# Attention in a fused transformer block: score buffers of three and four banks in turn, one bank for sums and turned sums

## What is computed

```
h = _layernorm(x) * (1 + ca) + sa
q, k, v = h @ Wq + bq, h @ Wk + bk, h @ Wv + bv          # 16 heads of 16
mask = cols <= rows + WINDOW                             # WINDOW = 128
scores = einsum('bhqd,bhkd->bhqk', q, k) / sqrt(16)
attn = softmax(where(mask, scores, -inf), axis=-1)
out = einsum('bhqk,bhkd->bhqd', attn, v)
x = x + ga * (out.transpose(...).reshape(b, s, d) @ Wo + bo)
```

## Time and profile before

| what | value |
|---|---|
| time, median of 3 runs | 1954.98 us (1951.56 to 1959.11) |
| the profiled execution | 1954.75 us |
| its span, first to last instruction | 1951.9 us |
| attention, first score matmul to last step | about 187 to 1260 us |
| PE busy over the span | 1763.1 us (90%) |
| ACT busy over the span | 1576.9 us (81%) |

### The profile page before, as it was taken

The page is one execution under the profiler, slowest core; times in us unless marked ns, Lnnn a source line. Parts: engine busy times, 40 slices in busy tenths (PEclk is TensorE's granted clock), DMA queues, the critical chain, the costliest instruction groups (busy, mean ns, idle before and its releaser), DMA issues. The chain is left out here.

```text
span 1951.9 us, 46416 instructions
## 1 busy us (share of the span) xinstructions
PE 1763.1 (90%) x18739; PEld 989.3 (51%) x18739; DVE 598.2 (31%) x1462; ACT 1576.9 (81%) x2077; POOL 266.1 (14%) x325
## 2 busy tenths in 40 slices
PE   7944999999999998999999999878399999999995
PEld 5732333333333333333333333266288888888884
DVE  6953000000000000000000000056466676776772
ACT  5623899999999998999999999834288888888882
POOL 1000100001010001000010000027312222222211
PEclk9965999999999999999999999977599999999998
DMA  5464400004000004000010000096422222222223
GB/s 178 146 161 107 93 10 10 10 10 88 23 11 10 10 12 92 10 10 10 10 27 18 10 2 2 26 369 221 144 36 36 37 39 36 37 39 37 37 39 100
DMA packets 83037, 112.47 MB, mean 58 GB/s; under 512 B 9340, under 2 KB 75836, under 8 KB 82236
## 3 DMA queue, kind: packets, MB, share of 16 engines
q1 hardware_dynamic: 65768, 86.65, 16.0%
q0 software_dynamic: 13296, 17.80, 5.4%
q10 hardware_dynamic: 3760, 5.03, 0.9%
HBM read 72.90 MB, written 40.74 MB: 58 GB/s over the span
## 5 line engine op out<-in xcount | busy, mean ns | idle before, releaser
L1144 ACT ACTIVATE at_probs<-at_scores 128x1536 f32<-128x1536 f32 (+2 forms) x756 | 1022.6, 1436 | 52.6 <-PE at_scores L1045 47.2
L1045 PE MATMUL at_scores<-at_q_rows,kept_k_rows 99*32 99x512 bf16 (+3 forms) x9920 | 616.0, 361 | 33.6 <-ACT at_probs L1144 17.0
L1062 PE MATMUL at_out<-at_probs,kept_v 128*17 128x512 f32 (+3 forms) x4832 | 586.1, 564 | 5.1 <-DVE at_out_T L1157 4.7
L1045 PEld LDWEIGHTS at_scores<-at_q_rows,kept_k_rows 99*32 99x32 bf16 x9920 | 238.1, 96 | 556.4 <-ACT at_probs L1144 344.6
L1157 DVE COPY at_out_T<-at_out 128x512 f32<-128x512 f32 x32 | 22.1, 691 | 967.0 <-PE at_out L1062 967.0
L1776 PE MATMUL ex_ps_y<-kept_w,kept_mixed 128*128 x1136 | 258.6, 381 | 2.4 <-ACT kept_mixed L1837 2.4
L1776 PEld LDWEIGHTS ex_ps_y<-kept_w,kept_mixed 128*128 128x128 f32 x1136 | 211.4, 191 | 28.9 <-issue 2.7
L1129 POOL TENSOR_SCALAR_AFFINE_SELECT at_probs<-at_probs 128x512 f32<-128x512 f32 (+2 forms) x156 | 83.0, 541 | 1003.9 <-ACT at_probs L1144 1001.9
L1837 ACT ACTIVATE kept_mixed<-ex_ps_hT,kept_b 128x128 f32<-128x128 f32 x568 | 154.6, 384 | 78.5 <-PE ex_ps_hT L1768 78.5
L1062 PEld LDWEIGHTS at_out<-at_probs,kept_v 128*17 128x17 f32 x4832 | 127.6, 98 | 130.0 <-DVE at_out_T L1157 20.4
L1862 DVE TENSOR_TENSOR ex_w_low<-kept_w,ex_w_high 128x1024 fp32r<-128x1024 f32 x142 | 167.7, 1222 | 39.1 <-ACT ex_w_high L1810 37.8
(11 more groups left out here) (232 smaller groups left out, 1252.1 us busy)
## 6 DMA issues: line engine op xcount, KB each, us to landing
kept_w<-in_W SPq DMA_DIRECT2D x16, 1024.0 KB, 14.8
kept_mixed<-queue SPq DMA_DIRECT2D x71, 129.5 KB, 2.1
k_parts<-kparts SPq DMA_DIRECT2D x8, 768.0 KB, 3.7
q_parts<-qparts SPq DMA_DIRECT2D x8, 768.0 KB, 3.7
at_q_rows<-q_parts SPq DMA_DIRECT2D x32, 192.0 KB
kept_k_rows<-k_parts SPq DMA_DIRECT2D x4, 1120.0 KB
x_rows<-in_x SPq DMA_DIRECT2D x4, 1024.0 KB, 13.8
kept_k_rows<-k_parts SPq DMA_DIRECT2D x8, 512.0 KB
```

The lines of the kernel that those rows point to most:

```text
L1045: ins = nc.tensor.matmul(ps_s[b:b + CT, c % 2, at:at + part], k_rows[:, k + b:k + b + CT], q_rows[:, q:q + part], start=True, stop=True)
L1062: ins = nc.tensor.matmul(ps_o[h * CT:h * CT + HD + 1, first:C], v[:, kb, g * GH + h, :], probs[:, slot, column:column + width], start=i == ...
L1144: nc.scalar.activation(probs[:, c % RING, 0:width], ps_s[:, c % 2, 0:width], ACT.Exp).then_inc(exped, 1)
```

## The change

`BANKS` becomes (3, 4). Chunks with an even running number use a PSUM buffer of three banks and those with an odd one a buffer of four. The exponentials get two rings of three slots, 3 and 4 banks wide. Chunks 0 and 1 of a tile keep their 1536 columns, whichever buffer they fall on. The cut of a tile into chunks now depends on the running number of its first chunk, so `place`, `pieces` and the others take the tile's number `r`. There are 663 chunks instead of 756: 284 of four banks, 356 of three, 9 of two and 14 of one.

The eight banks are now 3 + 4 + 1: the turned sums `ps_t` are a view of the bank of the sums. So the transposes of a tile may be written once its sums are copied, and the next tile's first step may be written only when DVE has read the turned sums. The first step waits for `normed` instead of `out_read`. In PE's order the transposes move from behind chunk 4 to behind chunk 3, where no steps are issued. The steps of chunks 0 and 1 both come behind chunk 4.

```
-        BANKS = 3
-        WIDE = BANKS * C
+        BANKS = (3, 4)
...
-        probs = sb("at_probs", [P, RING, WIDE], F32)
+        probs_of = [sb(f"at_probs_{n}", [P, RING // 2, n * C], F32) for n in BANKS]
...
-        ps_s = psum("at_scores", [P, 2, WIDE], F32)
+        ps_s = [psum(f"at_scores_{n}", [P, n * C], F32) for n in BANKS]
         ps_o = psum("at_out", [P, C], F32)
-        ps_t = psum("at_turn", [P, CB, P], F32)
+        ps_t = ps_o[:].rearrange("p (j q) -> p j q", j=CB)
...
+        def banks(c):
+            return BANKS[c % 2]
...
+            n, bank = 2, at // C
+            while bank >= banks(first_chunk[r] + n):
+                bank -= banks(first_chunk[r] + n)
+                n += 1
+            return n, bank * C
...
                 if i == 0 and r > 0:
-                    pe.wait_ge(out_read, r + 1)
+                    pe.wait_ge(normed, r)
...
                 pe.wait_ge(out_read, r + 2)
-
-                if r > 0:
-                    pe.wait_ge(normed, r)
                 for j in range(CB):
...
-                if n == LAG + 1 and c > LAG + 1:
+                if n == LAG and r > 0:
                     transposes(turn)
                     turn += 1
-                products(c - LAG + 1)
+                else:
+                    products(c - LAG + 1)
```

More of the change, by code:

```diff
@@ L951, in tile_steps @@
             return steps
-        def place(step, h):
-            at = step[3] + h * step[4]
[L956 to L982, removed]
@@ L984, in attention, with probs, place @@
-        order = [(g, tile, n) for g in range(G) for tile in range(NC) for n in range(chunks_of[tile])]
-        def edge_runs(tile, n):
+        def banks(c):
+            return BANKS[c % 2]
+        def probs(c):
+            return probs_of[c % 2][:, c % RING // 2]
+        def place(r, step, h):
+            at = step[3] + h * step[4]
+            if step[2] < 2:
+                return step[2], at
+            n, bank = 2, at // C
[3 more added lines that the diff above has]
+            return n, bank * C
@@ new lines, in attention, with pieces @@
+        tiles = [tile_steps(r % NC) for r in range(TILE_COUNT)]
+        first_chunk, first_step, chunks_of = [], [], []
+        for r, steps in enumerate(tiles):
+            first_chunk.append(sum(chunks_of))
+            first_step.append(sum(len(earlier) for earlier in tiles[:r]))
+            chunks_of.append(place(r, steps[-1], GH - 1)[0] + 1)
+        def pieces(r, n):
+            return [(i, h, place(r, step, h)[1]) for i, step in enumerate(tiles[r]) for h in range(GH)
+                    if place(r, step, h)[0] == n]
@@ L988, in edge_runs, with chunk_width, steps_begun @@
+        def chunk_width(r, n):
+            return sum(tiles[r][i][4] for i, _, _ in pieces(r, n))
+        def steps_begun(r, n):
+            return sum(place(r, step, 0)[0] <= n for step in tiles[r])
+        order = [(r, n) for r in range(TILE_COUNT) for n in range(chunks_of[r])]
+        def edge_runs(r, n):
             runs = []
-            for i, step in enumerate(tiles[tile]):
-                at = [column for k, h, column in pieces(tile, n) if k == i]
-                if step[0] > tile * CB and at:
+            for i, step in enumerate(tiles[r]):
+                at = [column for k, h, column in pieces(r, n) if k == i]
+                if step[0] > r % NC * CB and at:
@@ L992, in edge_runs, with masks_upto @@
                     runs.append((at[0], step[4], len(at)))
             return runs
[L995 to L1000, removed]
+        masks_of = [[len(edge_runs(r, n)) for n in range(chunks_of[r])] for r in range(TILE_COUNT)]
+        def masks_upto(r, n):
+            return sum(sum(m) for m in masks_of[:r]) + sum(masks_of[r][:n + 1])
@@ L1030, in _, with scores @@
         def _(pe):
-            def scores(g, tile, n, c):
+            def scores(r, n, c):
+                g, tile = r // NC, r % NC
                 if c >= 2:
@@ L1035, in scores @@
                 k_at, q_at = (g % 2) * GH * S, ((g * NC + tile) % Q_BUFFERS) * GH * C
-                for i, h, column in pieces(tile, n):
-                    kb, first, _, _, width = tiles[tile][i]
+                for i, h, column in pieces(r, n):
+                    kb, first, _, _, width = tiles[r][i]
                     done = 0
@@ L1044, in scores @@
                         for b in range(0, P, CT):
-                            ins = nc.tensor.matmul(ps_s[b:b + CT, c % 2, at:at + part], k_rows[:, k + b:k + b + CT],
+                            ins = nc.tensor.matmul(ps_s[c % 2][b:b + CT, at:at + part], k_rows[:, k + b:k + b + CT],
                                                    q_rows[:, q:q + part], start=True, stop=True)
@@ L1079, in _ @@
             for h in range(GH):
-                nc.tensor.matmul(ps_o[h * CT:(h + 1) * CT, :], zeros[:], probs[:, 0, 0:C], start=True, stop=False,
+                nc.tensor.matmul(ps_o[h * CT:(h + 1) * CT, :], zeros[:], probs(0)[:, 0:C], start=True, stop=False,
                                  skip_group_check=True)
-            pv = [0, 0, 0]
+            pv = [0, 0]
             def products(upto):
-                while pv[0] < G:
-                    g, tile, i = pv
-                    if chunk_base(g, tile) + place(tiles[tile][i], GH - 1)[0] >= upto:
+                while pv[0] < TILE_COUNT:
+                    r, i = pv
+                    if first_chunk[r] + place(r, tiles[r][i], GH - 1)[0] >= upto:
                         return
[L1091 to L1096, removed]
+                    product(r, i)
+                    pv[1] += 1
+                    if pv[1] == len(tiles[r]):
+                        pv[:] = [r + 1, 0]
             turn = 0
-            for c, (g, tile, n) in enumerate(order):
+            for c, (r, n) in enumerate(order):
                 if n == 0:
-                    if tile == 0:
-                        pe.wait_ge(k_in, (g + 1) * K_IN)
-                    r = g * NC + tile
+                    if r % NC == 0:
+                        pe.wait_ge(k_in, (r // NC + 1) * K_IN)
                     pe.wait_ge(q_in[r % Q_BUFFERS], (r // Q_BUFFERS + 1) * Q_IN)
-                scores(g, tile, n, c)
-                if n == LAG + 1 and c > LAG + 1:
+                scores(r, n, c)
+                if n == LAG and r > 0:
                     transposes(turn)
                     turn += 1
-                products(c - LAG + 1)
+                else:
+                    products(c - LAG + 1)
             for upto in range(len(order) - LAG + 1, len(order) + 1):
@@ L1117, in _ @@
         def _(pool):
-            for c, (g, tile, n) in enumerate(order):
-                for k, (column, spacing, count) in enumerate(edge_runs(tile, n)):
+            for c, (r, n) in enumerate(order):
+                for k, (column, spacing, count) in enumerate(edge_runs(r, n)):
                     if k == 0:
                         pool.wait_ge(exped, c + 2)
-                    part = probs[:, c % RING, column:column + (count - 1) * spacing + P]
+                    part = probs(c)[:, column:column + (count - 1) * spacing + P]
                     if count > 1:
-                        part = probs[:, c % RING, column:column + count * spacing].rearrange(
+                        part = probs(c)[:, column:column + count * spacing].rearrange(
                             "p (h q) -> p h q", h=count)[:, :, 0:P]
@@ L1152, in _ @@
                 g, tile = r // NC, r % NC
-                dve.wait_ge(pv_done, step_base(g, tile) + len(tiles[tile]))
+                dve.wait_ge(pv_done, first_step[r] + len(tiles[r]))
                 if r > 0:
```

30 lines of the change are left out of this document (14 added, 16 removed).

## The result

The changed kernel takes 1945.49 us (median of 14 runs, 1943.62 to 1949.77), the kernel before 1955.03 us beside it (14 runs, 1949.36 to 1960.18). The ratio is 0.9954, with a 95% interval of 0.9944 to 0.9965: about 9 us faster. The forecast was 1954 with 1942 to 1968 for 8 cases in 10, so the range holds the time, but the forecast's own range (1947 to 1961) does not. The profiled execution takes 1946.1 us with a span of 1944.4. Some 0.8 us of the gain lies outside the span: the time less the span is 1.7 us in the executions of the changed kernel and 2.5 in those of the kernel before, and no run here shows why.

The account below looks back on a forecast made before the run. The prediction took PE and ACT to share the bound, the time being PE's work plus its waits. Terms of -2 + 1 = -1 us on the profiled 1954.75 gave 1954 us, with 1942 to 1968 for 8 in 10.

Parts of the forecast that it names:

- The bound: In the attention, PE and ACT share the bound; the time is PE's work, which the change keeps, plus PE's waits.
- Term 1: Steady stretches of the attention: 0.455 us per bank against 0.456, over 2048 full banks, -2 us.
- term 2: A tile's beginning: PE waits 0.37 us instead of 0.35, chunk 5 starting 3.79 after chunk 3; 31 tile changes, +1 us.
- wide steps behind narrow chunks: At tile changes, 80 steps instead of 73 behind the first three chunks, at most 6 us; with 6.7 back, taken as nothing.
- The key loads: PE's three pauses in tile 2 of the first three groups, 11.0 us in all, left unchanged, 11 us each way.
- the pauses as a rival: Key-load pauses in tile 2 shift: gone gives 1943 us (chance 0.07), as much again 1965 (0.05).
- case of pauses gone: PE's key-load pauses in tile 2 vanish, giving 1943 us; chance 0.07.
- ACT as the bound: Steady stretches: seven banks take ACT's 3.10 us, 0.443 per bank, saving 27 us: 1928 us; chance 0.10.
- The longer chain: A tile's first step waits on copy, transposes, reciprocal and multiply, longer than the 1.46 us read: 1966 us; chance 0.15.
- the 4.7 us of the estimate: ACT's saving from 93 fewer exponentials at 0.051 us of PSUM access overhead each, by the Trainium skill's figure.

Follow-up runs that it names:

- 128 records: The kernel before with 32 one-column float32 matmuls and their weight loads added ahead of the attention: 1944.91 us, ratio 0.9957.
- the new order with its own bank: The changed kernel with two three-bank score buffers and a separate bank for the turned sums: 1950.77 us, ratio 0.9984 against the kernel before.
- 64 small matmuls: The kernel before with 64 small float32 matmuls (256 PE records with weight loads) added ahead of the attention: 1958.36 us, ratio 1.0026.

## Why the prediction came out as it did

**The bound** was read rightly: PE's work plus its waits. The kernels with chunk 1's steps moved show it best, since they change no instruction, only the order, and gain 9 us from waits alone.

**Term 1** (-2 us) and **term 2** (+1 us) stand in the trace at 12.73 us for 28 banks and 3.77 us for a tile's beginning. Term 1 lost by rounding: 0.456 less 0.455 is 0.001 a bank, but 10.95 / 24 less 12.73 / 28 is 0.0016, which over 2048 banks is 3.3 us and not 2. Together with "wide steps behind narrow chunks" at nothing the terms gave -1. Without the key loads the attention is 1.6 us shorter in the traces, and the kernels differ by 2.4 us in their medians, 0.0006 in their ratios, which can't be told from -1.

**The key loads** are the step that failed: "I leave them, with 11 us each way as bounds." The term was sized at 0 and measures about -7 by the medians, where the loads cost 16.8 us before and about 10 after, and -4 in the two traces. The prediction had the mechanism in a sentence ("only PE's place in its list decides which instructions are late") and even the pauses as a rival, but weighed it as a matter of chance at 0.12. It was also priced by the 11.0 us of idle time shown, and not with the slow clock and the late exponentials behind. The stated range holds 1945.49 us because it was drawn wide enough for the pauses to go; the sum of the terms does not explain it, and the case of pauses gone had a chance of 0.07. That the time lies in the range is in part luck.

That 128 records by themselves give the same 9 us shows that a shift of PE's list can be worth the whole gain. It does not show that a shift is what the change did. The first pause did not move, and the new order with three-bank buffers has the three places of the changed kernel and none of its gain. Only the third pause goes with the place: 2.44 and 2.70 us in these two, 4.74, 4.58 and 3.54 in the three kernels that stop about 10 matmuls earlier (before, the new order with its own bank, and 64 small matmuls). The first two pauses are 2.71 and 2.26 us with the wide chunks and 3.67 and 4.18 without, in one execution each. So it stays open how much of the smaller cost comes from the place in the list, from when PE gets there, and from chance. Nor is it shown why the changed kernel costs the same with 128 records more. Of its two places both cost 10 us or so; of the kernel before's three, one does.

**The rivals.** ACT as the bound (1928) is refuted by 12.73 us, not 12.4, for eight chunks. The longer chain (1966) is refuted by 1.47 us. The Trainium skill (Perfetto Trace Analysis, Optimizing Scalar/DVE Operations) says that breaking up instructions may help where ScalarE is not saturated but causes bubbles on other engines. That was not decisive here: 93 exponentials fewer came without the 4.7 us of the estimate in the kernels without loads (2.4 us by the medians), and without a loss.

## What to carry to other kernels

A pause of an engine for "issue" while a large load runs is a cost of the load, and an edit that only shifts the engine's list can shorten or lengthen it. Before a gain of half a per cent is put down to an edit, add idle instructions to the kernel before and see whether they give the same. Here cutting the load in pieces removed the pauses. The pauses are also the noisy part: look at a stretch without loads, such as the last head group here, to see what an edit does by itself. Where two engines are both near full, count the waits of each between two hand-overs, and move work out of the stretch in which one is late: that gave 9 us, where wider buffers with a shared bank gave 2.

## What the hardware showed beyond the forecast

By the counts, PE's records came in packets of 256 for 16 KB, one per 9.2 us in the attention (98 in 900 us). While a group's keys came in, at a DMA share of about 0.8, PE stopped for 1.4 to 4.7 us in most places of its list, and at the first stop of the kernel before no packet of q8 had come for over 12 us. With 0.92 for 4 us, and with 128 idle records ahead in the second group, it did not stop. After a stop of 3.35 us the granted clock of the next 4 us was 0.57, and so it was after one of 2.71 us; after stops of 2.84 and 2.90 us it stayed at 1.00.
